# A lower bound moved from the inverse root in SBUF to the summed squares in PSUM

## What is computed

```
def l2norm(t):
    return t / jnp.maximum(jnp.linalg.norm(t, axis=-1, keepdims=True), 1e-12)

qkv = x @ Wqkv                       # per layer, x shifted by one token in half its channels
q = l2norm(q) * qs;  k = l2norm(k) * ksc
q = q * cos * scale + rotate_half(q) * sin * scale
k = k * cos * inv   + rotate_half(k) * sin * inv
out = local_attention(q, k, v)       # scores, mask, softmax, times v
x = out @ Wo + x;  x = ffn_layer(shift_tokens(x), ...) + x
```

## Time and profile before

| | |
|---|---|
| median of 3 runs | 1865.2 us (1863.66 to 1868.27) |
| profiled execution | 1865.6 us, of which span of the program 1863.8 us |
| PE busy | 1804.9 us (97%) |
| DVE busy | 1531.7 us (82%) |
| ACT busy | 1455.7 us (78%) |
| POOL busy | 1359.5 us (73%) |

### The profile page before, as it was taken

The page is one execution under the profiler, slowest core; times in us unless marked ns, Lnnn a source line. Parts: engine busy times, 40 slices in busy tenths (PEclk is TensorE's granted clock), DMA queues, the critical chain, the costliest instruction groups (busy, mean ns, idle before and its releaser), DMA issues.

```text
span 1863.8 us, 67159 instructions
## 1 busy us (share of the span) xinstructions
PE 1804.9 (97%) x26763; PEld 1367.6 (73%) x26763; DVE 1531.7 (82%) x3002; ACT 1455.7 (78%) x2976; POOL 1359.5 (73%) x1165
## 2 busy tenths in 40 slices
PE   6999998999999999999999999999999999999997
PEld 4777776777777777777777777777777777777774
DVE  5776777788889888888888888888888888888886
ACT  5766665688788878888887888878878888887884
POOL 3010033899889888888888898889888888888880
PEclk9999999999999999999999999999999999999999
DMA  3000001344444444444443444444444444444342
GB/s 111 1 1 0 0 25 38 96 123 115 101 101 115 106 112 104 100 112 103 119 110 97 104 111 111 115 107 101 105 110 109 114 99 107 112 103 100 95 106 64
DMA packets 188251, 170.91 MB, mean 92 GB/s; under 512 B 20112, under 2 KB 187192, under 8 KB 187960
## 3 DMA queue, kind: packets, MB, share of 16 engines
q1 hardware_dynamic: 187960, 166.84, 35.9%
HBM read 21.01 MB, written 1.05 MB: 12 GB/s over the span
## 4 chain that ended last, share of the span: by engine, by line
PE 65%; ACT 12%; DVE 11%; issue 7%; POOL 4%; DMA 0%; SPq 0%; ACTq 0%; POOLq 0%; DVEq 0%
PE bank L1010 6%; PE bank L1051 6%; PE bank L978 6%; PE pair_bank L1029 5%; PE bank L1061 4%; PE bank L1113 3%; PE bank L1062 3%; PE bank L1063 3%; PE bank L1039 3%; PE bank L1135 3%; PE bank L896 2%; ACT sq L655 2%; DVE rot_v L1377 2%; ACT probs L735 2%; DVE rot_u L1376 2%
## 5 line engine op out<-in xcount | busy, mean ns | idle before, releaser
L436 POOL TENSOR_TENSOR z_norm<-probs_t,z_raw 128x512 f32<-128x512 f32 x376 | 480.9, 1279 | 101.2 <-DVE probs_t L1458 101.2
L442 POOL TENSOR_TENSOR z_raw<-rot_u,rot_v 128x512 f32<-128x512 f32 x384 | 498.3, 1302 | 70.8 <-DVE rot_v L1377 69.6
L1376 DVE TENSOR_TENSOR rot_u<-bank,tabs 128x512 f32<-128x512 f32 x384 | 262.9, 685 | 175.9 <-ACT sq L655 174.5
L1061 PE MATMUL bank<-x_high,w_high 128*128 128x256 f32 x768 | 302.1, 393 | 0.0
L469 POOL TENSOR_TENSOR sqs<-sq 128x512 f32<-128x512 f32 x192 | 246.3, 1283 | 60.5 <-issue 59.3
L1377 DVE TENSOR_TENSOR rot_v<-bank,tabs 128x512 f32<-128x512 f32 x384 | 261.1, 680 | 0.0
L1051 PEld LDWEIGHTS bank<-probs_t,v_late 128*64 128x64 f32 x3072 | 155.0, 137 | 144.5 <-issue 144.5
L655 ACT ACTIVATE sq<-bank 128x512 f32<-128x512 f32 x384 | 222.1, 593 | 24.1 <-PE bank L1063 17.7
L731 ACT ACTIVATE pair_bank<-pair_bank 128x512 f32<-128x512 f32 x192 | 111.7, 582 | 165.0 <-DVE pair_bank L1357 163.4
L664 ACT ACTIVATE probs_t<-bank 64x512 f32<-64x512 f32 x340 | 200.8, 591 | 22.7 <-PE bank L1039 20.7
L1063 PE MATMUL bank<-x_low,w_high 128*128 128x256 f32 x768 | 216.3, 282 | 0.0
(11 more groups left out here) (190 smaller groups left out, 4533.9 us busy)
## 6 DMA issues: line engine op xcount, KB each, us to landing
zqk<-z_norm SPq DMA_DIRECT2D x768, 128.0 KB
v_late<-v_sb SPq DMA_DIRECT2D x192, 192.0 KB, 2.6
w_stage<-in_L_ffn_Wqkv SPq DMA_DIRECT2D x24, 384.0 KB, 3.6
v_late<-v_sb SPq DMA_DIRECT2D x192, 32.0 KB, 2.2
wo<-in_L_ffn_Wo SPq DMA_DIRECT2D x24, 128.0 KB, 2.4
w<-in_L_ffn_W SPq DMA_DIRECT2D x12, 170.5 KB, 2.7
z_norm<-in_L_attn_x SPq DMA_DIRECT2D x4, 256.0 KB, 5.0
out<-z_raw SPq DMA_DIRECT2D x4, 256.0 KB, 2.3
```

The source lines that it names most:

```text
L436: return pool.tensor_tensor(z_norm[:, parity, idx, :, :], rinv(m)[:, idx, :].unsqueeze(1).broadcast_to([P, 2, T]), z_raw[:, parity, idx, : ...
L442: pool.tensor_tensor(z_raw[:, parity, idx, :, :], rot_u[:, idx, :, :], rot_v[:, idx, ::-1, :], ALU.add).then_inc(S[mark], 1)
L1061: pe.matmul(dst, w_high[:, r, j, cols], x_high[:, odd, :], start=True, stop=False)
L1376: dve.tensor_tensor(rot_u[:, idx, :, :], src, tabs[:, 2 * idx, :, :], ALU.mult)
```

## The change

The bound leaves the inverse root and is laid on the summed squares: DVE takes the maximum of bank B_N and a constant, in place in PSUM, right behind the key's rotation, between PE's `norms` and ACT's `Ln`. ACT's `Ln` waits for DVE and no longer for PE, and POOL waits for ACT and no longer for DVE.

```
# POOL, slot(s)
-                    pool.wait_ge(S["bound_ready"], s + 4)
+                    pool.wait_ge(S["rinv_ready"], s + 4)
...
# ACT, slot(s), m = s + 3
-                    act.wait_ge(S["n_done"], m + 1)
+                    act.wait_ge(S["bound_ready"], m + 1)
                     act.activation(ln_n(m), B_N[:, :].rearrange("p (a t) -> p a t", a=2), ACT.Ln, bias=tiny[:, 0:1], scale=LNS).then_inc(S["ln_done"], 1)
...
# DVE, slot(s)
                 if one:
                     rotate(s + 4, 1, B_K, "lk_done", "k_summed", "k_prod")
+                if two:
+                    dve.wait_ge(S["n_done"], s + 4)
+                    dve.tensor_scalar(B_N[:, :], B_N[:, :], 1e-24, None, ALU.max).then_inc(S["bound_ready"], 1)
                 if g == 0 and active(s, 8, 8 + GROUPS):
                     normed_out((s - 8) // G)
                 if three:
                     weigh_down(s)
-                if two:
-                    dve.wait_ge(S["rinv_ready"], s + 4)
-                    dve.tensor_scalar(rinv(s + 3), rinv(s + 3), 1e12 / ROOT, None, ALU.min).then_inc(S["bound_ready"], 1)
```

## The result

The change made the kernel slower: 2004.84 us (median of 4 runs, 2003.54 to 2004.95) against 1864.68 us (4 runs, 1863.66 to 1868.27), a ratio of 1.0746 with a 95% interval of 1.0728 to 1.0765. That is 140 us more. The forecast was 1994 us, 128 us more, in a range of 1930 to 2040.

The account below looks back on a forecast made before the run. The prediction took a DVE-ACT circle of mutual waits, close behind PE, to set the cost: 39.6 + 94.5 = 134 us over the slots, less 6 for the removed bound, gives 128 on 1865.6, so 1994 us, range 1930 to 2040.

Parts of the forecast that it names:

- The circle: DVE's query rotation and score shift, ACT's exponentials, `Ln`, output, squares and mask: each engine waits for the other, 338 us idle.
- 1.19 us in a slot where PE held nothing up: On ACT, `Ln` waits for shift, rotation and maximum, starting at 1643.84 in place of 1642.65, once per slot.
- E to H: Last four slots of the eight-slot period: growth 1.19, 1.19, 0.96 and 0.77, sum 4.11 us, 23 times in full.
- A to D: First four slots of the eight-slot period: together 1.65 us more, 24 times.
- the slack of 60 us: ACT's waits for PE before `Ln` (41.9 us) and the squares (17.7 us), 0.3 us a slot over 188 slots.
- the forecast's step for D: Slot D: ACT's waits for PE, 0.60 and 1.27 us, swallow ACT's own lag down to PE's 1.62 us.
- The price of the maximum: DVE's added 128x512 maximum in PSUM: 0.68 us taken, between 0.42 and 0.70; next instruction starts 0.60 us after it.
- the sum by slots: Growth over all slots: 24 x 1.65 + 23 x 4.11 = 134 us.
- The 6 us for L1458: Gain from removing DVE's old bound: about five slots near its longest, 1.2 us each, 6 us in all.
- Covered: Rival: PE stays the bound, the delay lies in idle time of ACT and DVE; 1865 us, chance 0.04.
- Faster, by the port: Rival: the PSUM form avoids the old bound's waits at SBUF, 27 us back at most; 1839 us, chance 0.04.
- Worse: Rival: later mask and weights hold up PE, or D absorbs nothing and layer turns add more; over 2028 us, chance 0.08.

Follow-up runs that it names:

- Off the chain: Against the kernel before: `Ln` waits for PE again, the old bound is left out, a no-effect maximum on bank B_K follows the key's rotation; 1893.29 us, ratio 1.0156.
- behind the weights: Against the kernel after: the maximum moved to behind `weigh_down` on DVE, `Ln` waits for it there; 2326.22 us, ratio 1.2476 to the kernel before.
- Twice: Against the kernel after: a second maximum behind the first, `Ln` waits for both; 2138.15 us, ratio 1.1457 to the kernel before.
- short: Against the kernel after: the maximum on 32 of the 512 columns, same order and waits; 1917.24 us, ratio 1.0276 to the kernel before.
- Late start: Against the kernel after: slots -3 to 0 keep the old bound on the inverse root; 1996.15 us, ratio 1.0695 to the kernel before.
- in the bias: Against the kernel before: no DVE bound, `Ln`'s small added constant raised to 1e-24 in its input's scale, POOL waits for ACT; 1847.22 us, ratio 0.9911.
- ahead of the rotation: Against the kernel after: the maximum stands ahead of the key's rotation on DVE, nothing else changed; 1975.81 us, ratio 1.0598 to the kernel before.

## Why the prediction was right

**What bounds the kernel: right.** The circle was on the page of before as 338 us of mutual waiting, behind a PE at 1250 of 1267 us. "Off the chain" and "behind the weights" show that `Ln`'s delay and not DVE's load sets the time: the same kind of instruction costs 29 us with `Ln` free of it, and 140 or 462 with `Ln` tied to it. "Twice" and "short" show the slope: a second maximum before `Ln` cost 133 us more, and 0.50 us less in the first gave back 88.

**1.19 us in a slot where PE held nothing up: right.** The table gives the distance from the start of L1355 in a slot to its start in the next, in us, read from DVE in order of time: the period that holds, from 1593.16 on, and the same one after, from 1713.52 on.

| slot | H | A | B | C | D | E | F | G | sum |
|---|---|---|---|---|---|---|---|---|---|
| before | 7.91 | 7.31 | 7.21 | 7.79 | 10.58 | 6.63 | 7.54 | 7.70 | 62.67 |
| after | 8.70 | 7.82 | 8.14 | 8.11 | 10.32 | 7.82 | 8.71 | 8.67 | 68.29 |
| grew by | 0.79 | 0.51 | 0.93 | 0.32 | -0.26 | 1.19 | 1.17 | 0.97 | 5.62 |
| forecast | 0.77 | 0.71 | 1.19 | 0.42 | -0.67 | 1.19 | 1.19 | 0.96 | 5.76 |

E to H come to 4.12 (forecast 4.11). A to D come to 1.50 (forecast 1.65, of which D is the rest of the sum: 1.65 - 0.71 - 1.19 - 0.42). Over the whole stream E to H grew by 93.6 us and A to D by 38.0, where the forecast had 94.5 and 39.6.

A to C came out smaller than forecast, and D took back less. In A (0.20 less) the query's rotation before stood behind DVE's own work, at 1607.18, and ACT's square had ended 0.16 us earlier: room that the forecast did not set off. B and C end with a wait of the next scores' maximum for PE. The one of 0.18 us the forecast took from C, where this table has it in B; a second one, of 0.20 us before the maximum of D, it left out, as it left such waits (14.7 us in all) out of the slack of 60 us. In D, ACT kept a wait of 0.40 us for the queries where the forecast had it swallowed (1.27 before), and gave back 0.41 us less. That this nearly evens out is what the forecast's step for D says: it brings ACT's lag down to PE's, whatever ACT's is. PE became late where the forecast had it, at the squares for L1157 in slot C (24 waits for `xc` above, one a period), and held ACT up in D:

```profile
1753.24 0.60 ACT L655 ACTIVATE sq<-bank 128x512 f32<-128x512 f32 x1 [0.40 <-PE bank L1063]
```

Counted from slot A's scores' maximum (L1355 at 1601.07 before, 1722.22 after), L1157 came 1.41 us later and the queries (L1061, at 1629.27 and 1751.93) 1.51, where the forecast had PE 1.62 late; A to D together grew by 1.50.

**The price of the maximum: right.** 0.68 was taken; the line alone shows

```profile
L1454 DVE TENSOR_SCALAR bank<-bank x192: 689/690/700, 304.0 to 1953.2; 128x512 f32<-128x512 f32 x192
```

and the next instruction starts 0.60 us behind it (1767.56 - 1766.96).

**The sum: 10 us low, by two terms.** From the first to the last L1355 the stream ran 1497.1 us before and 1628.7 after (the line alone, first that of before):

```profile
L1355 DVE TENSOR_REDUCE nm<-pair_bank x192: 678/682/694, 333.2 to 1830.3; 128x8 f32<-128x512 f32 x192
```

```profile
L1355 DVE TENSOR_REDUCE nm<-pair_bank x192: 678/681/693, 341.2 to 1969.9; 128x8 f32<-128x512 f32 x192
```

It grew by 131.6 us: between the 134 us of the sum by slots and the 128 us after its term for L1458. The rest of the 138.0 us between the spans is a term that the sum did not have: the stream starts 8.0 us later (341.2 - 333.2; behind its last L1355 the kernel is 1.6 us shorter). "For slots to 188" counted the slots with softmax. Slots -3 to 0 norm groups 0 to 3, and there DVE has the causal branch's last block ahead of the maximum. ACT after, in those slots, early in the stream:

```profile
304.69 0.69 ACT L735 ACTIVATE gate<-bank,tiny 128x512 f32<-128x512 f32 x1 [3.09 <-DVE bank L1454]
...
320.32 0.69 ACT L735 ACTIVATE gate<-bank,tiny 128x512 f32<-128x512 f32 x1 [3.09 <-DVE bank L1454]
```

`Ln` stands 3.09 us there, one slot takes 15.63 us, and before it took 12.03, with no such wait:

```profile
300.40 0.71 ACT L735 ACTIVATE gate<-bank,tiny 128x512 f32<-128x512 f32 x1
...
312.43 0.71 ACT L735 ACTIVATE gate<-bank,tiny 128x512 f32<-128x512 f32 x1
```

"Late start" took 8.7 us off by giving these slots alone their old order.

**The 6 us for L1458: not to be seen here.** Its full removal is worth 17 us ("in the bias"), three times the 6, but through two waits of PE. In the kernel after, the query's rotation waits for ACT's square in 186 of 192 slots (149 before), so a shorter DVE only lengthens that wait, as the prediction itself says before it takes the 6 us. Both errors go the same way: without this term and with the 8.0 us the sum would have been 142 us, where 140 were measured.

**The signs.** Foretold and seen: `Ln` waits some 200 us for L1454 (212.1), no wait of `Ln` for L1010 is left, DVE's wait for the square is longer, PE is at 92% with gaps that end on ACT, the period is 5 to 6 us longer, the clock in the steady stretch stays at 1.00. Not seen: PE busy near 1805 us; it is 1839.1. Of these 34 us, 32.8 lie between the first and the last L1355, for the same matmuls (1473.5 us before, 1506.3 after). L1073, L1039, L1149 and L1157, which now wait, hold 10.5 (busy times before: 109.1, 115.5, 29.6, 30.2; after: 113.4, 117.9, 31.4, 32.2); which lines hold the others stays open, and the ends of matmuls are modelled. Of the gaps that end on ACT the largest, 42.1 us, end on `gate` (L702), which the forecast did not name.

**The rivals.** "Covered" is out: `Ln` waits and PE has gaps. Nor does PE's own later start give much back: the maximum waited for PE's L1010 only twice, 2.8 us in all. "Faster, by the port": its 27 us of excess are near the 17 us that "in the bias" finds, but that kernel removes the instruction whole, so it doesn't tell a port from ordinary work in these 17 us. That the excess itself is a wait for POOL can be read in the trace of before: L1458 took over 500 ns 46 times, nearly all of the 27 us, and each of the 46 began while a POOL instruction was running and ended 0.28 us behind the end of a POOL instruction. The PSUM form runs at 689 to 700 ns where the SBUF form ran at 415 to 1600. The rule that the prediction cites from the Trainium skill, "SBUF — State Buffer", section "Who interferes with whom", would have it so, and the trace agrees with it. All that the bound's removal gave, 17 us, is an eighth of the 140 that the new order cost. "Worse" did not come, though its first part (weights late at PE's transposes) is there, at 21.6 us.

## What to carry to other kernels

Two engines that idle for each other are one circle, not slack: add up only the time in which a member waits for something outside it, and price a moved wait by how much later the waiting instruction starts, times the number of turns. An engine that takes its instructions in order passes a delay on even where it looks like the cause, so "it waits for PE anyway" is cover only if PE doesn't wait for the delayed engine within the turn, and if nothing that PE needs stands behind the wait on the same engine ("ahead of the rotation" missed by 46 us on that). And before an elementwise bound is moved to a better place, look for an instruction already there whose constant can take it: here that was the only version that won, 17 us. It lays the limit as a sum, which near the limit is not the same function as the maximum.

## What the hardware showed unexpectedly

**The clock fell where PE stood.** In the slots at the stream's start PE stood up to 4.1 us for `Ln` (the waits of PE above), and the stretch that follows one of these stands was granted 0.50, the lower of the two levels (1.2 of 2.4 GHz). Columns as in the earlier trace rows:

```profile
300.00:305.00 5.00, 1.30 (x13) 0.79 (x11) 3.37 (x9) 1.91 (x9) 0.88 (x1) 0.96 0.00 2
305.00:310.00 5.00, 4.57 (x21) 3.42 (x22) 2.15 (x6) 2.59 (x6) 4.27 (x5) 0.50 0.01 3
```

Part of the 8.0 us may therefore be PE at half speed; that was not tried by itself. In the kernel with the maximum behind the weights, where PE's `values` wait for `Ln` 156 times, up to 2.6 us each, the mean granted clock over most of the stream is lower too:

```profile
700.00:2200.00 1500.00, 1240.09 (x18567) 916.11 (x18568) 1000.79 (x1729) 944.82 (x1726) 994.34 (x831) 0.95 0.33 82
```

Its mean was 0.95 there, where it was 1.00 in the steady stretch of before and after. The 36 us by which that kernel passed its expectation may lie there in part; this was not tried by itself.
